# Pieces of the projections at three half groups in four and ahead of the sums at a unit's change; the preparation of the quantised weights started earlier

## The reference

```python
x = x + tanh(g_xattn[0]) * _L0_xattn_ref(_layernorm(x), ctx, ctx, ...)   # 16 heads, softmax, pruned
x = x + tanh(g_ffn[0])   * _L0_ffn_ref(_layernorm(x), w_gate, w_up, w_down)   # FP4 in blocks of 16
x = x + tanh(g_xattn[1]) * _L1_xattn_ref(ctx, _layernorm(x), ...)        # linear attention
x = x + tanh(g_ffn[1])   * _L1_ffn_ref(_layernorm(x), weight, bias)      # int8 per token

def _pruned_attention(q, k, v):
    scores = softmax(einsum('bhqd,bhkd->bhqk', q, k) / sqrt(D_K))
    col_sum = sum(scores, axis=2)                 # one sum a key
    _, idx = top_k(col_sum, int(S * 0.9))         # the lowest 52 of 512 keys are dropped
    ...
def fp4_quant_dequant(x):                         # of activations and of the three weights
    scale = max(max(abs(xb), axis=-1) / 6.0, 1e-12)
    q = _GRID[searchsorted(_MID, abs(xb / scale))] * sign(xb) * scale
```

## Time and profile before

| | |
|---|---|
| median of 3 runs | 1168.69 us (1166.48 to 1169.58) |
| profiled execution | 1172.58 us, its span 1170.9 us |
| mean granted TensorE clock | 0.962 |
| PE busy | 1052.1 us (90%) |
| DVE busy | 993.5 us (85%) |
| ACT busy | 897.6 us (77%) |
| POOL busy | 345.0 us (29%) |

### The profile page before, as it was taken

One profiled execution on the slowest core, in us unless ns is written; L12 is line 12 of the kernel. 1 busy time (PEld: TensorE's weight loads), 2 busy tenths in 40 slices (PEclk: granted clock), 3 DMA queues, 4 the chain that ended last, 5 costly groups with the idle time before them and its releaser, 6 DMA issues.

```text
span 1170.9 us, 17921 instructions
## 1 busy us (share of the span) xinstructions
PE 1052.1 (90%) x5580; PEld 474.5 (41%) x5580; DVE 993.5 (85%) x1903; ACT 897.6 (77%) x2032; POOL 345.0 (29%) x512
## 2 busy tenths in 40 slices
PE   7888999999999999999987777899999999999964
PEld 5332322322222322322321122346676777677642
DVE  7688888998898988988998947468999999999955
ACT  4577798999999999999999844765676677667644
POOL 7524123122122131131112886002222222222112
PEclk9897999999999999999998887999999999999986
DMA  8623421332233123303204101010121112110001
GB/s 278 144 68 78 127 61 33 101 97 75 59 101 96 44 71 100 93 19 100 69 26 110 56 16 40 10 46 27 28 63 37 46 36 59 42 46 19 28 9 37
DMA packets 76267, 75.99 MB, mean 65 GB/s; under 512 B 11860, under 2 KB 67980, under 8 KB 76172
## 3 DMA queue, kind: packets, MB, share of 16 engines
q1 hardware_dynamic: 76172, 74.84, 23.2%
HBM read 47.02 MB, written 27.28 MB: 63 GB/s over the span
## 4 chain that ended last, share of the span: by engine, by line
PE 55%; ACT 20%; DVE 15%; issue 6%; POOL 2%; DMA 1%; SPq 0%; DVEq 0%; ACTq 0%; POOLq 0%
PE ps_a L1733 13%; ACT ea L1440 9%; PE ps_b L1689 8%; PE ps_s L1292 8%; ACT prob L1454 6%; DVE nmax L1352 6%; PE ps_s L1312 3%; PE ps_s L1689 3%; PE ps_a L1254 3%; PE ps_b L1254 2%; PE ps_f L1704 2%; PE ps_a L1742 2%; PE ps_f L798 2%; PE ps_f L1767 2%; PE ps_f L769 1%
## 5 line engine op out<-in xcount | busy, mean ns | idle before, releaser
L1440 ACT ACTIVATE ea<-ps_a,nmax 128x512 f32<-128x512 f32 x512 | 354.0, 714 | 59.2 <-DVE nmax L1352 58.6
L1352 DVE TENSOR_REDUCE nmax<-ps_a 128x2 f32<-128x1024 f32 x256 | 311.6, 1219 | 53.5 <-PE ps_a L1254 51.4
L1292 PE MATMUL ps_s<-ea,rz 128*32 128x512 f32 x1024 | 259.9, 624 | 13.4 <-DVE rank L1381 11.4
L1312 PE MATMUL ps_s<-prob,v_pad 128*32 128x512 f32 x1024 | 256.2, 626 | 6.1 <-DVE att L1406 3.4
L1454 ACT ACTIVATE prob<-ps_b 128x1024 f32<-128x1024 f32 x214 | 226.8, 1060 | 4.5 <-PE ps_b L1254 4.0
L1733 PE MATMUL ps_a<-wgu,xT 128*128 128x352 f32 x512 | 166.3, 465 | 3.3 <-ACT xT L1898 2.1
L1254 PE MATMUL ps_b<-q_st,k_st 52*128 52x512 f16 x512 | 106.7, 393 | 34.2 <-ACT prob L1454 22.6
L1440 ACT ACTIVATION_READ_ACCUMULATOR ea<-ps_a,nmax 128x1 f32 x512 | 119.0, 232 | 0.0
L1254 PE MATMUL ps_a<-k_st,q_st 48*128 48x512 f16 x512 | 101.5, 393 | 14.6 <-ACT ea L1440 11.6
L1733 PEld LDWEIGHTS ps_a<-wgu,xT 128*128 128x128 f32 x512 | 92.9, 191 | 52.5 <-issue 10.3
L1910 ACT ACTIVATE ea<-ps_a 128x352 f32<-128x352 f32 x128 | 59.5, 466 | 59.1 <-PE ps_a L1733 58.9
(11 more groups left out here) (259 smaller groups left out, 1810.6 us busy)
## 6 DMA issues: line engine op xcount, KB each, us to landing
k_scr<-k_p SPq DMA_DIRECT2D x24, 256.0 KB, 3.4
q_scr<-q_p SPq DMA_DIRECT2D x24, 256.0 KB, 2.8
q_st<-q_scr SPq DMA_DIRECT2D x32, 192.0 KB, 5.0
k_st<-k_scr SPq DMA_DIRECT2D x32, 192.0 KB, 5.4
cT<-in_ctx_T SPq DMA_DIRECT2D x8, 512.0 KB, 5.2
x_in<-in_x SPq DMA_DIRECT2D x8, 512.0 KB, 6.3
c_in<-in_ctx SPq DMA_DIRECT2D x8, 512.0 KB, 4.5
v_scr<-v_s SPq DMA_DIRECT2D x8, 512.0 KB, 4.9
```

Of the source, the lines that this page charges most:

```text
L1292: e.matmul(ps_s[q:q + 32, :], rz[:, t, r, 2 * k + h, o:o + 32], ea[g % RING][:, 2 * k + h], start=(n == 0 and (apart or k == 0)), stop=(n ...
L1312: e.matmul(ps_s[o:o + 32, :], v_pad[u % 2][:, t, 4 * r + 2 * k + h], at.prob[g % PROBS][:, 2 * k + h], start=(t == 0 and (apart or k == 0) ...
L1352: e.tensor_reduce(nmax[u % 2][:, t].rearrange("p (h r) -> p r h", h=2)[:, r], ps_a[:, z % 2 * 2:z % 2 * 2 + 2], AX_X, ALU.max, negate=True ...
L1440: e.activation(ea[c % RING][:, g % 4], ps_a[:, g % 4], ACT.Exp, bias=nmax[u % 2][:, t, n:n + 1], accum_out=tot[u % 2][:, t, n:n + 1]).then ...
```

## The change

Three things. First, pieces 33 on stand in every half group from 42 whose number is not 1 modulo 4, three in four, where before they came at 0.7 a half group from 41. The last piece stands in half group 215 in place of 226. Second, at a unit's change (k = 4) PE's piece is written ahead of the column sums and values, in the others behind them as before. Third, the tables of the quantised weights: the loads at 230 in place of 235, the maxima, the twelve quarters and the eleven turns 3 to 12 half groups sooner, the last quarter's split at 262 in place of 273, the last turn at 272 in place of 283. DVE's copy of a turn stands one half group behind the turn and no longer in the same.

```diff
-LARGEST_AT = 241, 245, 249
+LARGEST_AT = 236, 238, 246
-QUARTER_AT = 243, 245, 247, 249, 251, 253, 255, 257, 259, 264, 267, 270, 273
+QUARTER_AT = 238, 240, 242, 244, 246, 248, 250, 252, 254, 256, 258, 260, 262
-TURN_AT = 253, 254, 255, 256, 261, 262, 263, 264, 277, 280, 283
+TURN_AT = 248, 250, 252, 254, 259, 261, 263, 265, 268, 270, 272
...
-    BEFORE, RATE = 33, 0.7
+    BEFORE = 33
+
+    OPENED = [z for z in range(OPEN, 256) if z % 4 != 1]
...
-        return OPEN + int((j - BEFORE) / RATE)
+        return OPENED[j - BEFORE]
...
-        def step(z):
+        def step(z, pieces):
...
+            changes = z % HALVES == 4
+            if changes:
+                pieces()
             g = within((z - 4) // 2, ALL_G)
             if g is not None:
                 for k in both(z, g // GROUPS < SUMS_APART, 1):
...
                 for k in both(z, g // TT >= VALUES_APART):
                     values(g, k)
+            if not changes:
+                pieces()
...
-    AHEAD, CLEAR, LOADS, OPENING = pj.ahead, 235, 244, 261
+    AHEAD, CLEAR, LOADS, OPENING = pj.ahead, 230, 244, 261
...
-                if z in TURN_AT:
-                    n = TURN_AT.index(z)
+                if z - 1 in TURN_AT:
+                    n = TURN_AT.index(z - 1)
                     fp4.copy(e, n, fp4_bank(n))
```

More of the change, by code:

```diff
@@ L2366, in _, with pieces @@
             for z in range(at.last):
-                step(z)
-                for s, part in pj.at_turn.get(z, ()):
-                    fill(s, part)
+                def pieces():
+                    for s, part in pj.at_turn.get(z, ()):
+                        fill(s, part)
+                step(z, pieces)
                 if z in TURN_AT:
```

## The result

Eight runs of the changed kernel have a median of 1177.56 us; without the one that was disturbed (1648.87 us) it is 1176.82 (1173.25 to 1182.0). The kernel before has 1169.13 on the same chip. The ratio, without the disturbed run, is 1.0058, with a 95% interval of 1.0033 to 1.0083: 6.8 us slower. I had said 1173.7, +5 us. The profiled execution took 1173.47 us with a span of 1171.7, the low end of its runs, and by chance only 0.8 us over the 1170.9 of before. The first 48 half groups hide the rest: unit 3 starts at 135.06 us for 142.40, and the granted clock of units 1 and 2 was 1.00 there, for 0.86 and 0.95 before. So I compare stretches that begin at a fixed half group, and the totals by their ratios.

The account below looks back on a forecast made before the run. PE, ACT and DVE bound half groups 48 to 224, none with 6% to spare; POOL's first root ends the quantisation. +6.5 + 0 - 1.5 = +5 us on the span: median 1173.7 us, range 1162 to 1181.

Parts of the forecast that it names:

- (a): Half groups 48 to 240: pieces at three in four cost +6.5 us on PE; bounds -4.6 and +10.
- (b): Order at a unit's change and what stands where: gain zero, waits 4.0 us a unit; bounds 6.5 gain, 7 loss.
- the break-even: Half groups 48 to 240: the new rate costs nothing only if waits fall from 4.05 to 3.4 us a unit.
- GRAM's wait of 1.4 us: Unit's change, one unit of two: GRAM, now ahead of the sums, waits 1.4 us for DVE's work on MM.
- the quiet half group: Half group without a piece before DVE's copy of the values: 1.35 us lost twice a unit, 2.7 us.
- packing the pieces throws away cover: Half groups 48 to 240: a piece costs PE 1.07 us; those without cannot beat ACT's 2.32 us; +6.5 us.
- The reorder at zero: Unit's change: moving PE's piece ahead of the sums costs 1.4 us in one unit of two, else nothing; gain taken as zero.
- (c): Quantisation of the weights sooner: 0 for POOL's operations up to its first root, bounds -5 and +5, and -1.5 for the turns.
- The load: Last load lands at 624.9 us; DVE waits some 5.5 us before the first maximum, half group 236.
- the load's wait runs through: Rival: DVE sets the quantisation's end, so its 5.5 us wait adds to +6.5: +10.5, 1179 us; chance 0.15.
- POOL's chain: POOL's operations to rs_a: start 5.7 us sooner, two splits +9.2, waits -4; with DVE's additions 0, bounds -5 and +5.
- The turns, -1.5: After 712.12 us: last three turns of weights leave PE's full stretch for half groups where it waits; -1.5, between 0 and -3.

Follow-up runs that it names:

- the tables by one: Against the kernel before: piece moved ahead of the sums, loads at 230, maxima and POOL's steps mostly one half group sooner, turns as before; ratio 0.9929.
- the later splits: Changed kernel with loads at 218 and the last splits of the down weights behind POOL's first root; ratio 0.9963 to the kernel before.

## Why the prediction was right, and where it was not

**(a) and (b), +6.5 us to half group 240.** The time is right: +6.2 to half group 236. Rate and reorder without the tables take 490.0 us from half group 48 to 240, where I had written 490.1 (the changed kernel's 498.5 has the load's wait in it). In the total they cost 4.4 us (1.0037), as POOL's first root comes 1.7 us sooner behind it. Right as well are the break-even at 3.4 us of waits a unit (4.2 measured is slower, 3.1 in the kernel with z % 4 == 2 free is faster), GRAM's wait of 1.4 us in every second unit, and the quiet half group ahead of the values' copy as a main loss, if at 1.1 us a unit and not 2.7 when it is moved away. My other reason was put too strongly: "packing the pieces throws away cover" is true of the 0.79 us each, but the kernel with the other free place packs as many pieces, and in this stretch it takes 442.2 us where the same reorder with the pieces at their old places takes 442.4 to 442.7. Up to half group 236 it is 1.3 us faster than they are on average. So the packing by itself costs nothing that can be seen here; it is the pattern with its gap at 1 of 4 that costs 11.5 us more than the one with it at 2.

**The reorder at zero.** This step failed. I held that in one kind of unit it gains nothing and in the other costs 1.4 us, because I looked only at whom GRAM would wait for. It is worth 7 us with the pieces at their old places and some 15 with the new ones. There the traces have 12.9 from half group 48 to 224: in five units a wait of 1.36 us takes the place of one of 2.04 (3.4 us in all); three of these five waits were followed by GRAM and scores at half the clock, 1.6 us more each (4.8); and the units in which I saw nothing to gain win 0.7 each (3.5), the last with pieces 1.2. The sum came out because I had also not charged the rate for this wait: two errors of one cause, on either side. To that extent it is luck that the +6.5 was met.

**(c) The load.** The landing was forecast at 624.9 and came at 625.23, by luck: the last transfer went out at 613.45, 1.8 us sooner than I had it, and took 2.2 us longer. The wait was forecast at 5.5 and came at 7.0, DVE being 1.2 us ahead. What failed is the step after it, that the wait is made good in POOL's stretch: without it the kernel is 4.7 us faster, give or take 3.6. This is the rival "the load's wait runs through", at some two thirds of its length by the ratios and less than half by the traces' fourth root. The heads cost nothing while the wait is there; with the tables by one, where it is gone, PE stands 4.31 us for them.

**(c) POOL's chain.** Sooner start: 5.0 us of 5.7. Waits: POOL's idle time inside the chain fell from 72.9 - 61.0 = 11.9 to 80.6 - 71.4 = 9.2 us, 2.7 of the 4; the magnitudes' part from 8.6 to 5.1. Two more splits: POOL's busy time rose by 10.4 us: 9.4 for the two splits by the lengths of their operations (my 9.2), 2.1 for two more parts of attention's shifts and values that now fall before the root, less about 1 since the other operations ran shorter. Sum +2.8 for my -0.5 and, with what DVE adds, 0; I had left out the attention's share. Counted from half group 229, as I had written it, the root is 4.1 us later, and the 3 us that I had allowed are missed. PE's wait of 5.22 us for the split is gone, as forecast. Two splits more alone moved the root by 6.4 us and the total by 3.6.

**The turns, -1.5.** Not confirmed. Put back they cost nothing that can be told.

Together, (c) is +2.5 us on rate and reorder (give or take 3.2 by the intervals), +2.9 on the reorder (2.8), +5.0 alone (1.4), where I had -1.5. In the traces it is small up to POOL's second root, 0.4, 0.9 and 0.5 us, and has grown to 2.9, 6.1 and 5.9 at the fourth; between the two the traces with the tables had the low clock and those without them had not. The kernel with the other free place has the same tables and the clock at full ahead of the third root, and its fourth root is at 202.7 us, as with the reorder alone, and 1.1 us behind that of rate and reorder. So my 0 for POOL's chain held to the second root, and what came behind it stood in no term of mine. In sum: +4.4 and +2.5 give the 6.8 us, forecast as +6.5 and -1.5: the total came out near because the first was too high and the second too low. The change is slower since its new places for the pieces cost more than its reorder wins, and, by its ratio with the loads at 218, since its load is asked for 7 us before it lands.

**What stays open.** The places with z % 4 == 2 free were not tried together with the load at 218 or the later splits, which by the table might win some us more. Why the three versions of the tables cost 2.5, 2.9 and 5.0 us is only partly the clock (below), and with one trace each this is argued, not shown. With twelve splits ahead of the root on the reorder alone, the fourth root is 4.4 us later with the clock at full ahead of the third.

## What to carry to other kernels

When work is moved ahead of a wait, ask not only what it waits for itself but what the engine would have waited for in its old place: here the work in front was covered by a wait that already had to be paid for. A wait for a transfer that stands in front of an engine's whole queue can run through to the end (here 3.0 to 4.7 us of 7.0), so fix the landing first and then the step that asks, and look at what the transfer has passed in its queue. In a periodic pattern try the place of the gap, and not only how many there are: one free index in four moved by one was 1.3% of the time, more than the 0.6% that the whole change cost, while from half group 48 to 224 three pieces in four half groups at the better place took as long as 0.7 a half group at the old ones.

## What the runs showed of the hardware

The granted clock of TensorE turned equal waits into unequal prices. From POOL's first root on, the kernel with reorder and tables and the kernel with the other free place run the same program. Their second to fourth roots, and their busy time in the 16 us that begin 152 us after half group 228, just ahead of the third; first reorder and tables:

```profile
717.41 1.07 POOL L1675 TENSOR_TENSOR rs_a<-ve_a,half 128x4 f32<-128x4 f32 x1 [6.96 <-DVE ve_a L2099]
758.38 1.01 POOL L1675 TENSOR_TENSOR rs_a<-ve_a,half 128x4 f32<-128x4 f32 x1 [23.97 <-DVE ve_a L2099]
796.02 1.02 POOL L1675 TENSOR_TENSOR rs_a<-ve_a,half 128x4 f32<-128x4 f32 x1 [7.07 <-DVE ve_a L2102]
```

```profile
739.24:755.24 16.00, 12.98 (x48) 4.33 (x40) 8.60 (x8) 10.77 (x15) 0.00 (x0) 0.68 0.04 9
```

```profile
744.65 1.09 PE L1254 MATMUL ps_b<-q_st,k_st 52*128 52x512 f16 x2 [2.30 <-ACT prob L1456]
745.68 1.93 PE L1312 MATMUL ps_s<-prob,v_pad 128*32 128x512 f32 x8
```

then z % 4 == 2 free:

```profile
717.96 1.07 POOL L1676 TENSOR_TENSOR rs_a<-ve_a,half 128x4 f32<-128x4 f32 x1 [6.53 <-DVE ve_a L2100]
755.80 1.01 POOL L1676 TENSOR_TENSOR rs_a<-ve_a,half 128x4 f32<-128x4 f32 x1 [22.20 <-DVE ve_a L2100]
791.23 1.02 POOL L1676 TENSOR_TENSOR rs_a<-ve_a,half 128x4 f32<-128x4 f32 x1 [7.06 <-DVE ve_a L2103]
```

```profile
740.57:756.57 16.00, 12.81 (x61) 4.67 (x60) 11.58 (x20) 12.71 (x21) 0.77 (x1) 1.00 0.04 10
```

```profile
743.84 0.88 PE L1255 MATMUL ps_b<-q_st,k_st 52*128 52x512 f16 x2 [2.30 <-ACT prob L1457]
744.64 1.06 PE L1313 MATMUL ps_s<-prob,v_pad 128*32 128x512 f32 x8
```

From the second root to the fourth they take 78.6 and 73.3 us. In both PE stood 2.30 us for ACT some 12 to 14 us before the third root; behind it the clock was at half in the first and at full in the second, and eight products of the values took 1.93 us in place of 1.06. All fourteen traces fall in two groups by the granted clock from 8 to 4 us ahead of the third root: 1.00 in six, whose next root comes 35.4 us later, and 0.50 to 0.59 in eight, whose next root comes 36.9 to 37.7 us later, the changed kernel's 37.5 among them. The four kernels with the old tables of the weights are all among the six, and of the ten with other tables eight have the low clock, so where the work stands seems to bear on it. But the same program from the first root on, with the same wait, came out both ways here, and so did the equal waits of 2.04 us within one trace, so the wait's length alone does not tell. The Trainium skill, "TensorE: Matmul & The Clock Gate", section "HAM oscillation — how this bites in real kernels", describes waits of PE after which the next products start at the half clock. The traces agree with that, and show it behind waits of 2.04 and 2.30 us, and that the same wait can also leave the clock alone.
